# A decoder step with two attentions, a mixture of low-rank experts and a quantised MLP on one core: score products by halves, keys by DMA, and all MLP inputs kept

## The chip, the cores and the metric

The kernel runs on one core of a Trainium2 chip. The metric is the device time of one execution in microseconds (us). A hand-written order for every engine is part of the program; the engines only meet at semaphores.

## The reference

Sixteen sequences of 128 positions with 256 features, all independent, go through five stages (`b` is the sequence, called a block below):

```python
a  = attention0(q=LN(x), k=ctx, v=ctx)         # 16 heads of 16, causal, softmax over 128 positions
x  = x + a
xh = LN(x)
x  = x + xh @ base_w.T + base_b + 2 * sum_e gate_e * (xh @ A_e) @ B_e   # top 2 of 8 experts, rank 16
q  = LN(x)
x  = x + gamma * attention1(q, ctx, ctx)       # over the features: 8 heads of 16 positions, 256 x 256 scores
xn = rmsnorm(LN(x)) * g
h  = gelu(bit_linear(xn, w1))                  # 256 -> 1024; inputs rounded to 8 bits, weights to -1, 0, 1
x  = x + bit_linear(h, w2)                     # 1024 -> 256
```

The second attention works on each block turned on its side: its positions are the 256 features, and its 8 heads have 16 of the 128 sequence positions each.

## The kernel before, in words

**Work of a block.** A head has only 16 rows to sum over, so scores are made with 32 rows of the systolic array at a time: `R = 32`, four row tiles `i = 0..3`, each with two heads (`E = 2`) side by side. The keys are kept with the rows of the other head set to zero: `k0` and `k1` hold for each `e` the 32 rows times the 0/1 column `keep[:, e]`. `place_k0` (L2348 to L2358) and `place_k1` (L2360 to L2371) make them on VectorE from `kv_in`, two `tensor_scalar` each per block.

A score is made twice. `scores0` (L1028) makes it with queries on partitions: four mask products by `mask_rows` (L1036), then the q by k product (L1046). `maxima0` (L2151) takes the row maximum on VectorE (L2154), negated. GpSimd splits the maxima in two bf16 halves (`split_max0`), TensorE turns them (`turn_max0`, L1058), ScalarE copies them (`copy_max0`), and `scores0_t` (L1062) makes the scores again with keys on partitions (L1071) and adds the negated maxima by a product with ones (L1076). ScalarE takes the exponential (`exp0`, L1662), GpSimd zeroes what the mask hides (`mask0`, L583), and `pv0` (L1125) multiplies by the values. The second attention has the same parts with a 1 for the 0: `scores1` (L1082, product L1090), `maxima1` (L2158, L2161), `turn_max1`, `scores1_t` (L1106, L1114 and the ones at L1119), `exp1` (L1710), `pv1` (L1139). It has no mask and twice the columns: its calls have two indices, `f` (or `k`) for half of the 256 columns and `h` for the half of the row tiles.

**Halves.** Every score call works on one half `h`: row tiles 0 and 1, or 2 and 3, in PSUM banks `at` and `at + 1`. `together(a, b)` (L1017) interleaves the matmuls of two calls on different halves, so that four row tiles are at work; a call given alone uses two. A block has 2 `scores0`, 2 `scores0_t`, 4 `scores1` and 4 `scores1_t`, so 192 calls in all; 130 of them stand in 65 pairs.

**The expert stage.** `turn_xh1`, `ff` (L1176, product L1182: base weights, all A and the router in one), `logits_`, `top_`, `index`, `gate1_`, `pick`, `gates_`, `gated_` on VectorE, `turn_gated`, `lora` (L1193), `moe_out`.

**The second attention's denominators.** They stand in the rows of `u1`, four heads apart, and are brought to the right rows through HBM by SyncE (SP): `save_u1` (L360) writes `u1`, `close_z1` (L366, two DMAs) reads back the denominators, `rz1_` (L2247) inverts them on VectorE, `save_rz1` writes them, `spread_rz1` (L389) reads them spread over the rows, and `close_u1` (L376, two DMAs) reads the sums. `a1_` (L645, GpSimd) multiplies the two, and `out_` (L2253) adds it to the stream. All of SP's instructions wait in program order.

**The MLP.** `xn_`, `amax_in`, `scale_in`, `round_in` (ScalarE), `quant_in`, `turn_in`, `copy_in` prepare a block's input `xq_t`; there are `XT_BUFS = 7` buffers. `up` (L1206), `gelu` (L1741), `amax_hid`, `keep_amax_hid` (GpSimd), `scale_hid`, `round_hid`, `quant_hid`, `turn_hid`, `copy_hid`, `down` (L1225), `scale_output`, `add_output` and `store_out` follow. The gelu needs another activation table than the exponential, so the MLP comes after all the attention work: inputs 0 to 6 are made before it, 7 to 15 in it. Its hidden rows have their own buffer `hid`, and the MLP weights come in f32 into `w1_sb` and `w2_sb`, are summed (`weight_sum`), rounded on ScalarE (`round_weight`) and clipped (`clip_weight`) among the first blocks.

**Order.** Each engine's program is a flat list of calls, written out from L410 (SP), L699 (GpSimd), L1233 (TensorE), L1768 (ScalarE) and L2385 (VectorE). From block 4 of the expert stage on it repeats. One turn of TensorE's list is, for instance:

```python
turn_xh1(8, 7); pv0(9, 0, 6); pv0(9, 1, 6)
together(scores0_t(9, 0, 0), scores1(5, 1, 1, 2)); turn_in(2, 7); ff(8, 6); turn_q0(12, 5)
together(scores1_t(4, 0, 0, 0), scores0(11, 1, 2)); turn_u0(9, 7); turn_max1(5, 5); pv1(4, 0, 4)
together(scores1(6, 0, 1, 0), scores1_t(5, 1, 0, 2)); pv1(4, 1, 4); turn_gated(8, 7)
together(scores1(6, 0, 0, 0), scores1_t(5, 1, 1, 2)); together(scores1(6, 1, 0, 4)); lora(8, 6)
turn_max0(10, 7); together(scores0(11, 0, 0), scores1_t(5, 0, 1, 2)); together(scores0_t(10, 1, 4))
```

(It is condensed to several calls on a line, with a label or two moved to one turn.) It has five pairs and two single calls.

Of the kernel before, what the change touches and what calls it, by code (L numbers as in the profile page):

```python
# [55 lines left out]
XT_BUFS = 7  # L56
HID_BUFS = 7
CONSTS = 15
TURNS = 4
# [22 lines left out]
def program(nc, x, kv, w_ff, base_b, router_b, lora_b, attn_gamma, w1, w2, mlp_gamma, out):  # L82
    with ExitStack() as ctx:
# [17 lines left out]
        ones_bf = sb("ones_bf", [P, P], BF16)  # L101
        warm = sb("warm", [P, 1])
# [4 lines left out]
        keep = sb("keep", [P, E])  # L107
        attn_gamma_all = sb("attn_gamma_all", [P, 1])
        mlp_gamma_all = sb("mlp_gamma_all", [P, D])
        w1_sb = sb("w1_sb", [P, FT * HID])  # L110
        w2_sb = sb("w2_sb", [P, HT * D])
# [8 lines left out]
        k0 = sb("k0", [P, K0_BUFS, FT, E, P])  # L120
# [70 lines left out]
        hid = sb("hid", [P, HID_BUFS, HID])  # L191
# [26 lines left out]
        kv_landed = [sem(f"kv_landed{n}") for n in range(KV_BUFS)]  # L218
        keep_ready = sem("keep_ready")
        k0_placed = sem("k0_placed")  # L220
        k1_placed = sem("k1_placed")
        v0_ones = sem("v0_ones")
# [112 lines left out]
        def _(sp):  # L335
# [74 lines left out]
            load_kv(0)  # L410
            load_kv(1)
            load_x(0)
            load_x(1)
            load_x(2)
            load_kv(2)
            load_weight(0)
            load_x(3)
            load_weight(1)
            load_x(4)
            load_x(5)  # L420
            load_constants()
            load_kv(3)
            load_kv(4)
            load_kv(5)
            load_kv(6)
            load_kv(7)
            load_kv(8)
            save_u1(0)
            close_z1(0)
            close_u1(0)  # L430
            save_rz1(0)
            spread_rz1(0)
            load_kv(9)
            save_u1(1)
            close_z1(1)
            close_u1(1)
            save_rz1(1)
            spread_rz1(1)
            load_kv(10)
            save_u1(2)  # L440
            close_z1(2)
            close_u1(2)
            save_rz1(2)
            spread_rz1(2)
            load_kv(11)
            save_u1(3)
            close_z1(3)
            close_u1(3)
            save_rz1(3)
            spread_rz1(3)  # L450
            load_kv(12)
            save_u1(4)
            close_z1(4)
            close_u1(4)
            save_rz1(4)
            spread_rz1(4)
            load_kv(13)
# [2538 lines left out]
```

## Time and profile before

| what | value |
|---|---|
| three runs | 369.82, 373.1 and 378.56 us; median 373.1 |
| the profiled execution | 373.23 us |
| its span, first to last instruction | 371.2 us, so 2.0 us lie around it |
| TensorE busy | 327.1 us (88%) |
| VectorE busy | 291.4 us (78%) |
| ScalarE busy | 234.1 us (63%) |
| GpSimd busy | 202.5 us (55%) |
| mean granted TensorE clock | 0.974 of 2.4 GHz |

The busy time of an engine is the union of its instructions' times. Durations below are of this one execution. A row of a timeline that says x8 is a run of eight instructions merged, and its two numbers are the start of the first and the time to the end of the last. Each f32 product shows as two records, one for each of its passes.

### The profile page before, as it was taken

The page shows a single profiled execution, that of the slowest core. Times are in us where ns is not written, and L with a number is a line of the kernel's source. Part 1 is how long each engine was busy: PE and PEld are TensorE (multiplying, and loading weights), DVE is VectorE, ACT ScalarE, POOL GpSimd, SP SyncE. Part 2 cuts the span into 40 slices and gives each one's busy share as a digit, 9 for nine tenths or more (in the row PEclk, how much of TensorE's full clock was granted, in tenths as well). Part 3 has the DMA queues.
Part 4 walks back from the last instruction along what each step waited for, and adds up shares of the span by engine and source line. Part 5 has one row for each costly group of instructions (what it writes and reads, how often), then busy time and mean ns, then how long its engine had stood idle before and what let it go on. Part 6 is the DMA issues. An engine that isn't in the chain of part 4 may idle for free.

```text
span 371.2 us, 10692 instructions
## 1 busy us (share of the span) xinstructions
PE 327.1 (88%) x3730; PEld 211.8 (57%) x3730; DVE 291.4 (78%) x691; ACT 234.1 (63%) x373; POOL 202.5 (55%) x443
## 2 busy tenths in 40 slices
PE   0799799899999999989999999989999999498774
PEld 0477556557566666657666575756645563265543
DVE  6784786886869888888989888786887755689992
ACT  1225535347575676757576675656656669689992
POOL 7537784545355647564654747555643332455554
PEclk9999969899999999999999999999999999889998
DMA  7900211000212120221112021011111112021111
GB/s 246 354 26 3 63 52 29 2 3 2 58 33 59 33 72 18 75 55 51 59 32 65 26 74 44 24 40 31 47 44 32 48 58 61 17 77 52 45 57 57
DMA packets 20276, 20.61 MB, mean 56 GB/s; under 512 B 6016, under 2 KB 15872, under 8 KB 20224
## 3 DMA queue, kind: packets, MB, share of 16 engines
q1 hardware_dynamic: 20224, 19.94, 17.4%
q8 instruction: 30, 0.49, 0.6%
q14 instruction: 22, 0.18, 0.2%
HBM read 13.51 MB, written 6.42 MB: 54 GB/s over the span
## 4 chain that ended last, share of the span: by engine, by line
PE 47%; DVE 18%; issue 12%; DMA 11%; POOL 4%; ACT 4%; SPq 1%; POOLq 0%; DVEq 0%; ACTq 0%
PE ps L1090 6%; PE ps L1071 5%; PE ps L1114 5%; PE ps L1182 5%; PE ps L1046 4%; DMA u_kept<-u 4%; DMA rz_kept<-rz 4%; PE ps L1036 4%; DVE max L2161 3%; PE ps L1134 3%; DVE max L2154 2%; PE ps L1195 2%; PE ps L1147 2%; PE ps L1229 2%; ACT p L1710 2%
## 5 line engine op out<-in xcount | busy, mean ns | idle before, releaser
L1710 ACT ACTIVATE p<-ps 128x1024 f32<-128x1024 f32 x64 | 65.0, 1024 | 57.7 <-PE ps L1119 57.3
L2161 DVE TENSOR_REDUCE max<-ps 128x4 f32<-128x1024 f32 x64 | 76.9, 1219 | 14.6 <-PE ps L1090 14.5
L1090 PE MATMUL ps<-k,q 32*128 32x512 f32 x256 | 66.0, 641 | 6.9 <-DVE max L2161 4.8
L1114 PE MATMUL ps<-q,k 32*128 32x256 f32 x512 | 70.6, 398 | 0.6 <-DVE max L2161 0.5
L2154 DVE TENSOR_REDUCE max<-ps 128x8 f32<-128x1024 f32 x32 | 38.8, 1217 | 14.2 <-PE ps L1046 14.2
L1114 PEld LDWEIGHTS ps<-q,k 32*128 32x128 f32 x512 | 44.4, 184 | 8.6 <-issue 3.3
L1662 ACT ACTIVATE p<-ps 128x1024 f32<-128x1024 f32 x32 | 32.6, 1018 | 20.2 <-PE ps L1076 20.0
L583 POOL TENSOR_SCALAR_AFFINE_SELECT p<-p 128x1024 f32<-128x1024 f32 x32 | 35.2, 1100 | 13.4 <-ACT p L1662 13.2
L1046 PE MATMUL ps<-k,q 32*128 32x256 f32 x256 | 39.9, 444 | 1.8 <-DVE k L2357 1.8
L1071 PE MATMUL ps<-q,k 32*128 32x128 f32 x512 | 38.0, 297 | 0.4 <-DVE max L2154 0.4
L1147 PE MATMUL ps<-p,v 128*32 128x256 f32 x512 | 34.3, 384 | 3.5 <-ACT p L1710 3.5
L1071 PEld LDWEIGHTS ps<-q,k 32*128 32x128 f32 x512 | 34.3, 203 | 3.9 <-DVE max L2154 2.1
L1090 PEld LDWEIGHTS ps<-k,q 32*128 32x128 f32 x256 | 19.3, 183 | 17.2 <-issue 7.4
L1046 PEld LDWEIGHTS ps<-k,q 32*128 32x128 f32 x256 | 24.8, 214 | 3.8 <-DVE k L2357 2.0
L1036 PE MATMUL ps<-mask_rows,ident_rows 32*128 32x512 bf16 (+3 forms) x256 | 26.1, 328 | 0.5 <-ACT p L1710 0.2
L649 POOL TENSOR_TENSOR a<-uz,rz_all 128x256 f32<-128x256 f32 x16 | 11.7, 733 | 26.8 <-issue 26.8
L1182 PE MATMUL ps<-wff_sb,xh_t 128*128 128x392 f32 x64 | 26.1, 532 | 0.0
L1229 PE MATMUL ps<-w_q,hq_t 128*128 128x256 bf16 x128 | 18.0, 287 | 8.1 <-DVE hq_t L2335 6.6
L1147 PEld LDWEIGHTS ps<-p,v 128*32 128x32 f32 x512 | 14.4, 109 | 18.4 <-issue 12.3
L1119 PE MATMUL ps<-max_t,ones_bf 2*128 2x512 bf16 x128 | 24.9, 376 | 0.0
L612 POOL TENSOR_SCALAR var<-mv 128x1 f32<-128x1 f32 x32 | 7.6, 239 | 30.3 <-DVE mv L2245 20.1
L1754 ACT ACTIVATE hr<-hid,round_all,qscale 128x1024 f32<-128x1024 f32 x16 | 20.0, 1250 | 4.9 <-DVE qscale L2323 3.3
(134 smaller groups left out, 727.4 us busy)
## 6 DMA issues: line engine op xcount, KB each, us to landing
kv_in<-in_kv SPq DMA_DIRECT2D x16, 256.0 KB, 2.8
u_kept<-u SPq DMA_DIRECT2D x16, 256.0 KB, 3.1
w_sb<-in_w SPq DMA_DIRECT2D x4, 512.0 KB, 7.6
uz<-u_kept SPq DMA_DIRECT2D x32, 64.0 KB
rz_all<-rz_kept SPq DMA_DIRECT2D x16, 128.0 KB
out<-xs SPq DMA_DIRECT2D x16, 128.0 KB, 1.7
xs<-in_x SPq DMA_DIRECT2D x1, 768.0 KB, 10.3
xs<-in_x SPq DMA_DIRECT2D x2, 256.0 KB, 5.8
```

The source lines that it names most:

```text
L583: pool.affine_select(out=kept, in_=kept, compare_op=ALU.is_ge, fill=0.0, base=0, pattern=[[0, HALF * FT * E], [1, P]], channel_multiplier= ...
L1036: pe.matmul(heads, ident_rows[rows, a, :], mask_rows[rows, a, a * R:P].unsqueeze(1).broadcast_to([R, FT * E, P - a * R]), start=(a == 0), ...
L1046: last = pe.matmul(ps[:, at + m, f * D:(f + 1) * D], q0[rows, b % Q_BUFS, f, :], k0[rows, n, f, :, :].rearrange("p e l -> p (e l)"), start ...
L1071: pe.matmul(ps[:, at + m, c * P:(c + 1) * P], k0[rows, n, f, e, :], q0[rows, b % Q_BUFS, f, :], start=(c == 0), stop=True, skip_group_chec ...
L1090: pe.matmul(ps[:, at + m, :], q1[rows, b % Q_BUFS, f * P:(f + 1) * P], k1[rows, n, :, :].rearrange("p e l -> p (e l)"), start=True, stop=True,
L1114: pe.matmul(ps[:, at + m, e * D:(e + 1) * D], k1[rows, n, e, k * P:(k + 1) * P], q1[rows, b % Q_BUFS, :], start=(e == 0), stop=True, skip_ ...
L1147: last = pe.matmul(ps[R * j:R * (j + 1), at, h * D:(h + 1) * D], v1[:, b % V1_BUFS, k * H1 + h * G + j, :], p1[:, k, h * HALF + m, e, :], ...
L1182: last = pe.matmul(ps[:, at, 0:NFF], xh1_t[:, f, :], wff_sb[:, f, :], start=(f == 0), stop=(f == FT - 1), skip_group_check=True)
L1662: act.activation(p0[:, b % 2, h * HALF:(h + 1) * HALF, :, :, :].rearrange("p i f e q -> p (i f e q)"), wide(at).rearrange("p m c -> p (m c ...
L1710: act.activation(p1[:, k, h * HALF:(h + 1) * HALF, :, :].rearrange("p i e q -> p (i e q)"), wide(at).rearrange("p m c -> p (m c)"), ACT.Ex ...
L2154: dve.tensor_reduce(max0[:, h * HALF:(h + 1) * HALF, :].rearrange("p i c -> p (i c)"), wide(at).rearrange("p m (c k) -> p (m c) k", k=P), ...
L2161: dve.tensor_reduce(max1[:, f, h * HALF:(h + 1) * HALF, :].rearrange("p i e -> p (i e)"), wide(at).rearrange("p m (e k) -> p (m e) k", k=D ...
```

## The change

It does five things, and orders all five engines' lists anew.

1. **First keys by DMA.** `place_k0` goes. Three `memset`s zero `k0` at the start; SP then loads each block's keys straight from HBM by two DMAs (`load_k0`), one for each head of a pair, each to every second partition of the 128, 1 KB a row. The layout of `k0` is now `[n, e, f, l]`, and the rows of the two heads alternate, so `norm0` writes its output permuted (stride of two elements), and the products read `k0[rows, n, :, f, :]`. A `load_k0(b)` waits until `scores0_t` of block `b - 3` is done with the buffer; `kv_in` no longer waits for `place_k0`.
2. **Second keys by one product.** `place_k1`'s two `tensor_scalar` of 256 columns become one `tensor_tensor` of 2 x 256, both operands broadcast.
3. **Halves in pairs in other places.** `together` is unchanged. The two halves of one `scores0` are paired for blocks 0 to 5 and 7, and sometimes two `scores1` or two `scores1_t` of different halves. The whole list has 63 pairs and 66 single calls. The products with ones stay, in `scores0_t` and in `scores1_t`.
4. **16 MLP inputs.** `XT_BUFS` goes from 7 to 16. To make room, `hid`, `w1_sb` and `w2_sb` share one buffer. Inputs 0 to 12 are turned before the first gelu (`round_in(13)` also stands before it), and 13 to 15 after it.
5. **SP.** x comes first, then the first keys, the constants, `kv_in` and the MLP weights; `close_u1` goes ahead of `close_z1`; `TURNS` (semaphores in rotation) goes from 4 to 3.

The diff, cut to its core (the lists show the start, one turn and the beginning of the MLP):

```diff
-XT_BUFS = 7
+XT_BUFS = 16
 HID_BUFS = 7
-TURNS = 4
+TURNS = 3
...
+        wide_rows = sb("wide_rows", [P, HID_BUFS * HID])
+        w1_sb = wide_rows[:, 0:FT * HID]
+        w2_sb = wide_rows[:, FT * HID:2 * FT * HID]
+        hid = wide_rows[:, :].rearrange("p (n c) -> p n c", c=HID)
...
-        k0 = sb("k0", [P, K0_BUFS, FT, E, P])
+        k0 = sb("k0", [P, K0_BUFS, E, FT, P])
...
-                    sp.wait_ge(k0_placed, (b - KV_BUFS + 1) * E)
-                    sp.wait_ge(k1_placed, (b - KV_BUFS + 1) * E)
+                    sp.wait_ge(k1_placed, b - KV_BUFS + 1)
...
+            def load_k0(b):
+                n = b % K0_BUFS
+                if b < K0_BUFS:
+                    sp.wait_ge(k0_zeroed, b + 1)
+                else:
+                    for h in range(2):
+                        sp.wait_ge(st0_ready[h], (b - K0_BUFS + 1) * HALF)
+                heads = kv[b, :, 0, :].rearrange("(i e d) l -> e i d l", e=E, d=DH)
+                for e in range(E):
+                    sp.dma_start(k0[e:P:E, n, e, :, :].rearrange("p f l -> p (f l)"), heads[e]).then_inc(k0_landed[n], 16)
...
+            load_x(0); load_x(1); load_x(2); load_k0(0); load_x(3); load_k0(1); load_k0(2); load_constants()
+            load_x(4); load_kv(0); load_kv(1); load_x(5); load_kv(2); load_weight(0); load_weight(1)
...
+            save_u1(4); load_kv(12); close_u1(4); close_z1(4); load_k0(12); save_rz1(4); spread_rz1(4)
...
-                pe.wait_ge(k0_placed, (b + 1) * E)
+                pe.wait_ge(k0_landed[n], (b // K0_BUFS + 1) * E * 16)
...
-                                         k0[rows, n, f, :, :].rearrange("p e l -> p (e l)"), start=False, stop=True,
+                                         k0[rows, n, :, f, :], start=False, stop=True,
...
+            together(scores0(0, 0, 0), scores0(0, 1, 2)); turn_q0(1, 7); turn_max0(0, 7)
+            together(scores0(1, 0, 0), scores0(1, 1, 2)); together(scores0_t(0, 1, 4)); together(scores0_t(0, 0, 0))
+            turn_q0(2, 7); turn_max0(1, 7); together(scores0(2, 0, 0), scores0(2, 1, 2)); ...
...
+            together(scores1_t(4, 0, 0, 0), scores0(9, 1, 2)); pv0(8, 0, 6); pv0(8, 1, 6); pv1(4, 0, 5)
+            turn_max1(5, 4); turn_u0(8, 6); together(scores1_t(5, 1, 0, 0), scores1(6, 1, 1, 2))
+            turn_gated(7, 4); turn_max0(9, 6); pv1(4, 1, 5)
+            together(scores1(6, 1, 0, 0), scores1_t(5, 0, 1, 2)); together(scores1(6, 0, 0, 4)); lora(7, 7)
+            together(scores1_t(5, 1, 1, 0), scores0(10, 0, 2)); together(scores0_t(9, 1, 4)); turn_xh1(8, 7)
+            together(scores1(6, 0, 1, 0)); together(scores0_t(9, 0, 2)); ff(8, 7); turn_in(3, 6); turn_q0(11, 5)
...
-                normalise(xh0[:, :], stream(b), rstd0[:, b:b + 1], shift0[:, b:b + 1]).then_inc(norm0_done, 1)
+                turns = xh0[:, :].rearrange("p (t d e) -> p t e d", e=E, d=DH)
+                normalise(turns, stream(b).rearrange("p (t e d) -> p t e d", e=E, d=DH), rstd0[:, b:b + 1],
+                          shift0[:, b:b + 1]).then_inc(norm0_done, 1)
...
-                for e in range(E):
-                    dve.tensor_scalar(k1[:, n, e, :], kv_in[:, b % KV_BUFS, 1, :], keep[:, e:e + 1], 1.0, ALU.mult,
-                                       ALU.mult).then_inc(k1_placed, 1)
+                dve.tensor_tensor(k1[:, n, :, :], kv_in[:, b % KV_BUFS, 1, :].unsqueeze(1).broadcast_to([P, E, D]),
+                                  keep[:, :].unsqueeze(2).broadcast_to([P, E, D]), ALU.mult).then_inc(k1_placed, 1)
...
+            round_in(13); gelu(0, 0, 7); gelu(0, 1, 4); gelu(1, 0, 6); gelu(2, 0, 5); gelu(1, 1, 4); gelu(3, 0, 7)
+            round_hid(0)
```

In the list before, eight gelus stand ahead of `round_hid(0)`, and no `round_in` right ahead of them.

## Rows read from the trace of the kernel before

**Rows 1.** Busy time by stretch: PE, PEld, DVE, ACT, POOL, clock, DMA share, GB/s.

```profile
11.50:43.00 31.50, 30.85 (x262) 21.48 (x262) 21.42 (x47) 14.22 (x19) 16.34 (x34) 1.00 0.30 97
43.00:55.30 12.30, 10.29 (x111) 6.58 (x112) 11.34 (x30) 4.07 (x7) 10.78 (x19) 0.72 0.26 65
55.30:106.00 50.70, 47.88 (x581) 31.36 (x577) 38.28 (x84) 28.94 (x49) 23.93 (x52) 0.97 0.07 19
106.00:237.60 131.60, 125.94 (x1704) 85.02 (x1702) 111.36 (x287) 89.79 (x150) 79.69 (x177) 1.00 0.17 49
237.60:309.70 72.10, 67.37 (x730) 39.94 (x728) 51.64 (x133) 45.74 (x68) 32.89 (x77) 1.00 0.15 46
309.70:371.20 61.50, 44.76 (x358) 27.46 (x354) 48.66 (x93) 49.20 (x78) 30.11 (x62) 0.93 0.14 48
```

**Rows 2.** Timeline of PE in one turn of the repeating part.

```profile
198.12 0.59 PE L1090 MATMUL ps<-k,q 32*128 32x512 f32 x2
...
199.08 0.70 PE L1195 MATMUL ps<-lora_b_sb,gated_t 128*128 128x256 f32 x2
...
201.12 0.27 PE L1071 MATMUL ps<-q,k 32*128 32x128 f32 x2
...
202.33 0.44 PE L1165 MATMUL ps<-ident,xh 128*128 128x128 f32 x2
...
203.71 0.38 PE L1071 MATMUL ps<-q,k 32*128 32x128 f32 x2
...
205.02 0.28 PE L1202 MATMUL ps<-ident_bf,xq 128*128 128x128 bf16 x2
```

**Rows 3.** Timeline of PE: `ff` of blocks 4 and 12.

```profile
105.99 1.58 PE L1182 MATMUL ps<-wff_sb,xh_t 128*128 128x392 f32 x4
...
237.62 1.58 PE L1182 MATMUL ps<-wff_sb,xh_t 128*128 128x392 f32 x4
```

**Rows 4.** Timeline of PE: its longest wait in the turn of rows 2.

```profile
197.16 0.70 PE L1090 MATMUL ps<-k,q 32*128 32x512 f32 x2 [0.41 <-DVE max L2161]
```

**Rows 5.** Timeline of PE in the first 60 us.

```profile
35.73 1.25 PE L1036 MATMUL ps<-mask_rows,ident_rows 32*128 32x512 bf16 x8
36.77 2.02 PE L1046 MATMUL ps<-k,q 32*128 32x256 f32 x8
...
46.75 0.48 PE L1046 MATMUL ps<-k,q 32*128 32x256 f32 x2 [1.81 <-DVE k L2357]
...
55.83 1.08 PE L1046 MATMUL ps<-k,q 32*128 32x256 f32 x8
```

**Rows 6.** Timeline of DVE: a memset, and the first-key products.

```profile
4.92 1.34 DVE L2380 MEMSET v<- 128x1536 f32 x1 [0.27 <-issue]
...
45.48 1.21 DVE L2357 TENSOR_SCALAR k<-kv_in,keep 128x256 f32<-128x256 f32 x2
```

**Rows 7.** Groups of VectorE: xcount | busy, mean ns of one | idle before.

```profile
L2357 DVE TENSOR_SCALAR k<-kv_in,keep 128x256 f32<-128x256 f32 x32 | 15.8, 538 | 0.1
L2370 DVE TENSOR_SCALAR k<-kv_in,keep 128x256 f32<-128x256 f32 x32 | 11.5, 404 | 4.1 <-PE ps L1119 4.0
L2257 DVE TENSOR_TENSOR xs<-a,xs 128x256 f32<-128x256 f32 x16 | 7.4, 465 | 8.4 <-POOL a L649 8.4
```

**Rows 8.** Timelines of SP, POOL and ACT where the MLP begins.

```profile
310.75 1.08 SPq L382 DMA_DIRECT2D uz<-u_kept  x2
...
310.79 4.96 ACT L1747 ACTIVATE hid<-ps,dequant 128x512 f32<-128x512 f32 x8
...
317.43 0.72 POOL L649 TENSOR_TENSOR a<-uz,rz_all 128x256 f32<-128x256 f32 x1 [4.60 <-issue]
...
318.57 1.24 ACT L1754 ACTIVATE hr<-hid,round_all,qscale 128x1024 f32<-128x1024 f32 x1 [2.83 <-DVE qscale L2323]
```

**Rows 9.** A group of ScalarE (columns as rows 7); a DMA issue: KB, us to landing.

```profile
L1739 ACT COPY xq_t<-ps 128x256 bf16<-128x256 bf16 x16 | 5.8, 381 | 0.0
...
xs<-in_x SPq DMA_DIRECT2D x1, 768.0 KB, 10.3
```

More of the change, by code:

```diff
@@ new lines, in _ @@
+            together(scores0_t(4, 0, 0))
+            lora(1, 7)
+            together(scores1(0, 1, 1, 2), scores1(0, 1, 0, 4))
+            turn_q0(6, 6)
+            together(scores1(0, 0, 0, 0))
+            turn_max0(5, 7)
+            together(scores1(0, 0, 1, 4))
+            pv0(3, 0, 6)
+            pv0(3, 1, 6)
+            together(scores0(6, 0, 2), scores0_t(5, 1, 0))
+            turn_u0(3, 7)
+            turn_max1(0, 6)
+            together(scores1(1, 1, 1, 0), scores1(1, 1, 0, 4))
@@ new lines, in _ @@
+            turn_xh1(5, 6)
+            together(scores1_t(2, 1, 1, 0))
+            ff(5, 7)
+            together(scores1(3, 0, 1, 2), scores0_t(6, 0, 4))
+            turn_in(0, 6)
+            together(scores1_t(2, 0, 0, 0))
+            turn_max0(7, 5)
+            turn_q0(8, 6)
+            pv0(6, 0, 4)
+            pv0(6, 1, 4)
+            pv1(2, 0, 6)
+            turn_max1(3, 5)
+            turn_u0(6, 4)
+            together(scores1_t(3, 1, 0, 0), scores1(4, 1, 1, 2))
+            turn_gated(5, 5)
@@ L1395, in _ @@
-            together(scores0(11, 0, 0), scores1_t(5, 0, 1, 2))
-            together(scores0_t(10, 1, 4))
-            turn_xh1(8, 7)
+            pv1(4, 0, 5)
+            turn_max1(5, 4)
+            turn_u0(8, 6)
+            together(scores1_t(5, 1, 0, 0), scores1(6, 1, 1, 2))
+            turn_gated(7, 4)
+            turn_max0(9, 6)
+            pv1(4, 1, 5)
+            together(scores1(6, 1, 0, 0), scores1_t(5, 0, 1, 2))
+            together(scores1(6, 0, 0, 4))
+            lora(7, 7)
@@ L1416, in _ @@
-            together(scores0_t(11, 1, 4))
-            turn_xh1(9, 7)
+            pv1(5, 0, 5)
+            turn_max1(6, 4)
+            turn_u0(9, 6)
+            together(scores1_t(6, 1, 0, 0), scores1(7, 1, 1, 2))
+            turn_gated(8, 4)
+            turn_max0(10, 6)
+            pv1(5, 1, 5)
+            together(scores1(7, 1, 0, 0), scores1_t(6, 0, 1, 2))
+            together(scores1(7, 0, 0, 4))
+            lora(8, 7)
+            together(scores1_t(6, 1, 1, 0), scores0(11, 0, 2))
@@ L1425, in _ @@
[L1425 to L1437 removed]
+            pv1(6, 0, 5)
@@ new lines, in _ @@
+            turn_max1(7, 4)
+            turn_u0(10, 6)
+            together(scores1_t(7, 1, 0, 0), scores1(8, 1, 1, 2))
+            turn_gated(9, 4)
+            turn_max0(11, 6)
+            pv1(6, 1, 5)
+            together(scores1(8, 1, 0, 0), scores1_t(7, 0, 1, 2))
+            together(scores1(8, 0, 0, 4))
+            lora(9, 7)
+            together(scores1_t(7, 1, 1, 0), scores0(12, 0, 2))
+            together(scores0_t(11, 1, 4))
+            turn_xh1(10, 7)
+            together(scores1(8, 0, 1, 0))
@@ new lines, in _ @@
+            turn_u0(11, 6)
+            together(scores1_t(8, 1, 0, 0), scores1(9, 1, 1, 2))
+            turn_gated(10, 4)
+            turn_max0(12, 6)
+            pv1(7, 1, 5)
+            together(scores1(9, 1, 0, 0), scores1_t(8, 0, 1, 2))
+            together(scores1(9, 0, 0, 4))
+            lora(10, 7)
+            together(scores1_t(8, 1, 1, 0), scores0(13, 0, 2))
+            together(scores0_t(12, 1, 4))
+            turn_xh1(11, 7)
+            together(scores1(9, 0, 1, 0))
+            together(scores0_t(12, 0, 2))
@@ new lines, in _ @@
+            together(scores0_t(14, 1, 4))
+            turn_xh1(13, 7)
+            together(scores1(11, 0, 1, 0))
+            together(scores0_t(14, 0, 2))
+            ff(13, 7)
+            turn_in(8, 6)
+            together(scores1_t(10, 0, 0, 0), scores0(15, 1, 2))
+            pv0(14, 0, 6)
+            pv0(14, 1, 6)
+            pv1(10, 0, 5)
+            turn_max1(11, 4)
+            turn_u0(14, 6)
+            together(scores1_t(11, 1, 0, 0), scores1(12, 1, 1, 2))
+            turn_gated(13, 4)
```

2106 lines of the change are left out of this document (1008 added, 1098 removed).

## The prediction

> **What bounds the kernel now.** I read the busy table first: TensorE is busy for 88% of the span, VectorE for 78%, and no other engine for over 63%. An average over a start, a repeating part and an MLP says little, so the second view is the busy time by stretch [rows 1]. From 106 to 237.6 us TensorE works 125.9 of 131.6 us, and VectorE 111.4. In the MLP from 309.7 on it is ScalarE (49.2 of 61.5) and VectorE (48.7) that are full, and TensorE is not. In the first 55 us TensorE looks full as well, but its work is slow: eight q by k records take 2.02 us at 36.8 us and 1.08 us at 55.8 us [rows 5]. That is the 1.2 GHz level against the 2.4 GHz level. The granted-clock column does not show it in the stretch from 11.5 us to 43 us (it says 1.00) and shows it from 43 to 55.3 us as 0.72 [rows 1]; so I go by the durations.
>
> Third, the timeline of one turn of the repeating part [rows 2, 4]. Eight turns lie between the `ff` of block 4 and that of block 12 [rows 3]: 131.63 / 8 = 16.45 us a turn. TensorE idles (131.6 - 125.94) / 8 = 0.71 us of each [rows 1], 0.41 of it behind `maxima1` [rows 4]. TensorE therefore bounds the repeating part, with VectorE as its partner in a loop. What a freed VectorE can give back there is at most the 0.71 us a turn.
>
> **Part 1, first keys by DMA.** It takes 32 `tensor_scalar` off VectorE, 15.8 us in all [rows 7], about 1 us a block. In the repeating part that shortens nothing by itself, since TensorE is the bound. At the start it does: at 45.5 us the keys of blocks 3 to 5 stand in VectorE's queue [rows 6], and TensorE waits 1.81 us for them [rows 5]. Afterwards the clock falls back: 0.72 over 12.3 us means that 0.56 of it, 6.9 us, ran at half speed, some 3.4 us lost. With the wait gone I take back 1.8 us and a third of the 3.4, together -2.9 us; the bounds are 0 (another wait takes the place; the weight rounding and clipping move to this spot) and -5.2. What is added: three memsets of 512 columns, a third of 1.34 us each [rows 6], 1.3 us on VectorE while GpSimd is still building the masks, so nothing. `norm0` writes with a stride; ScalarE is idle for over a third of every stretch before the MLP, so nothing there either. Each block's two DMAs are issued by SP after `close_z1`, two turns before the keys are read. No row shows this DMA. The nearest are x's loads in the crowded first 20 us, the slowest of which took 10.3 us to land [rows 9]. The first keys are issued at about 3 us and wanted at about 12, so the bounds are 0 and +1.5; I take 0. A `load_k0` waits for `scores0_t` three blocks before, and behind it stand `save_rz1` and `spread_rz1`; those wait for the denominators anyway, which come 1 to 2 us later.
>
> **Part 2, second keys by one product.** Before, two of them cost 11.5 / 16 = 0.72 us a block [rows 7]. One product of 2 x 256 isn't in the trace. The nearest is a `tensor_tensor` of 256 columns, 0.465 us [rows 7]; the new one lies between that and twice that. I take the middle, 0.70: no change, bounds -0.25 and +0.21 us a block on an engine that isn't the bound.
>
> A rule speaks against this part. The Trainium skill, VectorE: DVE Perf Modes, section "Mode 2x_2P — use both read ports for one tensor", says that f32 `tensor_scalar` gets two elements a cycle from SBUF and `tensor_tensor` never does. The trace agrees in kind: 0.404 against 0.465 us for 256 columns [rows 7]. The same page gives (N + 151) / 0.96 ns for an f32 `tensor_tensor`, an estimate of 0.69 us here; the sum would not move by it.
>
> **Part 3, pairs in other places.** The number of score calls stays; 65 pairs become 63. At the start the two halves of `scores0` run as one. One half takes from 35.7 to 38.8 us at the slow clock [rows 5], 3.06 us, and a pair should take about as long. But the maxima, their split and the turn stand behind each, so TensorE idles after block 0's scores instead. Walking the new list with these durations I come to the turned maxima of block 2 at about 41 us in place of 43: -1.8 us, bounds -4 and 0.
>
> In the repeating part the new turn has four pairs and four single calls in place of five and two. A pair of `scores0_t` and `scores1` takes 205.02 - 203.71 = 1.31 us [rows 2]. Alone, `scores1` takes 199.08 - 198.12 = 0.96 and `scores0_t` 202.33 - 201.12 = 1.21 [rows 2]. In the new turn they follow each other on different halves, so the second pass of the first (0.48) can lie beside the second: 0.96 + 1.21 - 0.48 = 1.69, +0.38 us a turn, bounds 0 and +0.86 (no overlap). Against it stands the idle time. In the new order `turn_max0` and `pv1` lie between a `maxima1` and the claim of its bank, so the 0.41 goes; `turn_max1` now has only `turn_u0` between it and the product that needs its copy, which ScalarE makes after an exponential, a norm and a copy. I expect 0.25 us of waiting a turn there and nothing else: -0.46. Sum -0.08 a turn, eight turns: -0.6 us, bounds -3.7 and +5.
>
> From 55.3 to 106 us TensorE idles 50.7 - 47.88 = 2.8 us [rows 1] in much the same loops, with VectorE 76% full. A lighter VectorE gives a part of it back: -1 us, bounds -3 and +1. From 237.6 to 309.7 the idle 4.7 us [rows 1] come from waits for exponentials, which the change leaves: 0, bounds -2 and +1.
>
> **Parts 4 and 5, MLP and SP.** Six `copy_in` (blocks 7 to 12) leave the stretch in which ScalarE is the bound: 6 x 5.8 / 16 = -2.2 us [rows 9]. The MLP's first waits are given by SP, though: `a1_(14)` waits 4.60 us for its DMAs, `keep_amax_hid(0)` stands behind it on GpSimd, and ScalarE waits 2.83 us for the scale [rows 8]. The change issues `close_u1`, 1.08 us for its two DMAs [rows 8], ahead of `close_z1`, which is first in the chain of DMAs that ends last: +1.1. `out_(14)` goes ahead of `scale_hid(0)` on VectorE: +0.4. Eight gelus took 4.96 us ahead of the first rounding [rows 8]; now six stand there, so two come after the wait instead of beside it: +1.2. Sum +0.5 us, bounds -2.5 and +4; the upper one because `round_in(13)`, which needs `a1_(13)`, now stands ahead of the first gelu. `TURNS` = 3 only lengthens a wait that is three blocks old: nothing. The shared `hid` buffer adds no wait, for the weights are clipped 250 us before.
>
> **The sum.** -2.9 - 1.8 - 0.6 - 1.0 + 0 + 0.5 = -5.8 us. The profiled execution took 373.2 us, the same as the median of the three runs (373.1, which range from 369.8 to 378.6). Forecast: 367.5 us (the sum rounded), 1.5% faster. About 2% is what a measurement of this kernel can tell from no change.
>
> **Rivals.** (A) *Most of the idle time and all of the fall-back of the clock go.* The idle time from 43 to 309.7 us is 2.0 + 2.8 + 5.7 + 4.7 = 15.2 us [rows 1]; with half of it back, 3.4 us for the clock, 1.8 at the start, and the lost pair paid (+3), the time is 373.2 - 7.6 - 3.4 - 1.8 + 3.0 = 363.4. For it: VectorE has 1 us a block more slack, and most of TensorE's waits name VectorE. Against it: the repeating part idles only 4%. Chance 0.35.
>
> (B) *The repeating part gets longer.* The place is the product after `turn_max1`. If ScalarE is late there by one exponential (1.0 us) and the two single calls do not overlap (+0.86), a turn takes 16.45 + 1.0 + 0.86 - 0.41 = 17.9 us. Eight turns give +11.6, the start -2: 382.8. It decides from a turn of about 17.6 us on. For it: fewer pairs, and a wait with only 0.5 us of cover. Against it: ScalarE is 68% busy there [rows 1]. Chance 0.12.
>
> (C) *The change doesn't do all that it says.* The products of ones stay in the code, so no TensorE work goes; that is certain and is in my sum. Left over is the case in which the start gains nothing, because the maxima's chain and not the scores sets it, and the MLP loses 3 us to SP's chain: 373.2 - 0.6 + 3 = 375.6. Chance 0.10.
>
> My own case has 0.43, from 365 to 371. Over the cases: faster by over 2% (below 365.7) 0.37, within 2% 0.50, slower (above 380.6) 0.13. The range 359 to 377 leaves out most of B and the far end of A.
>
> **What would show the steps right or wrong.** The `ff` of blocks 4 and 12 should stand 131 us apart (129 to 135). The first should come at about 100.5 in place of 106.0. There should be no wait of TensorE for a key product near 45 us, and the clock of 43 to 55 us should be above 0.8. VectorE's busy time should fall by about 15 us, to 276, and the new key product should take about 0.70 us. From the first gelu to the end it should be about 60.5 us as before, with ScalarE's wait ahead of the first rounding longer than 2.8 us. I am wrong if a turn takes over 17 us, or if TensorE waits for key DMAs at the start.

## The result, and the profile after

The changed kernel takes 366.5 us (median of 20 runs, 364.3 to 374.1), the kernel before 371.8 us (20 runs, 368.4 to 384.3). The ratio is 0.984, with a 95% interval from 0.981 to 0.986: 1.6% faster. Eleven of the twenty runs of the changed kernel lie between 364.3 and 366.8 us and nine between 370.9 and 374.1; the ratio compares the faster group of the one kernel with that of the other. The forecast was 367.5 us, so the sum came out right. Its terms did not, as the profile shows at once. The profiled execution of the changed kernel has a span of 363.4 us, 7.8 less than before.

The first view is the busy time by stretch, with the columns of [rows 1]. The first two stretches are those of before, the third is six turns from the first product with the second values (`pv1`, line 1177) of block 3 to that of block 9, the last is from the first gelu to the end:

```profile
11.50:43.00 31.50, 26.07 (x368) 18.43 (x367) 23.30 (x44) 16.58 (x25) 23.60 (x46) 0.89 0.52 180
43.00:55.30 12.30, 9.62 (x115) 6.17 (x113) 10.49 (x32) 6.93 (x13) 7.48 (x13) 1.00 0.18 55
131.21:232.86 101.65, 97.46 (x1282) 64.71 (x1280) 81.36 (x199) 68.66 (x114) 60.15 (x132) 1.00 0.17 53
307.01:363.40 56.39, 40.21 (x345) 25.59 (x350) 46.34 (x81) 46.16 (x70) 27.00 (x58) 0.97 0.15 50
```

The same two last stretches of the kernel before, cut at its own marks:

```profile
143.57:242.09 98.52, 94.32 (x1275) 63.41 (x1275) 83.49 (x215) 66.68 (x111) 58.92 (x132) 1.00 0.17 49
310.79:371.20 60.41, 43.67 (x350) 26.95 (x348) 47.67 (x90) 48.12 (x77) 30.11 (x62) 0.93 0.15 49
```

Three things are to be seen. TensorE did 368 matmul records in the stretch from 11.5 to 43 us, in 26.1 us of busy time, where before it had done 262 in 30.9 [rows 1]: it is much faster there although it idles more. A turn then takes 101.65 / 6 = 16.94 us, against 98.52 / 6 = 16.42 before: the repeating part got longer by 0.52 us a turn. (`start_unpaired`, `save14_late` and `changed_again` have the same lists in this stretch and the same clock, and take 16.76, 16.98 and 16.99 us, so the tenth of a us is not firm.) The MLP takes 56.4 us in place of 60.4.

`pv1` comes once a block in both kernels and serves as a mark (its first half, start in us). Its place within a turn differs a little between the two orders, so single rows are good to some us:

| | block 0 | 3 | 6 | 9 | 12 | first gelu | end |
|---|---|---|---|---|---|---|---|
| before | 93.6 | 143.6 | 193.1 | 242.1 | 283.3 | 310.8 | 371.2 |
| after | 85.2 | 131.2 | 182.5 | 232.9 | 276.3 | 307.0 | 363.4 |
| lead | 8.4 | 12.4 | 10.6 | 9.2 | 7.1 | 3.8 | 7.8 |

The start gives 12.4 us by block 3, the rest of the attention gives 8.6 of them back, and the MLP adds 4.0. The timeline of TensorE tells of the start:

```profile
18.06 0.40 PE L1088 MATMUL ps<-ident_bf,max_split 128*128 128x128 bf16 x4 [2.69 <-POOL max_split L626]
19.09 2.04 PE L1076 MATMUL ps<-k,q 32*128 32x256 f32 x16
...
22.54 1.16 PE L1101 MATMUL ps<-q,k 32*128 32x128 f32 x16
...
27.29 1.94 PE L1076 MATMUL ps<-k,q 32*128 32x256 f32 x16
...
29.06 1.05 PE L1101 MATMUL ps<-q,k 32*128 32x128 f32 x16
...
40.07 1.08 PE L1076 MATMUL ps<-k,q 32*128 32x256 f32 x14
```

Both halves of a score, 16 records, take 2.04 us at the 1.2 GHz level, as long as one half of 8 records took before (2.02) [rows 5]. And the 2.4 GHz level comes sooner, though not at one stroke. The turn of 18.06 us is at it already (0.40 us, where the same four records take 0.61 at the lower level), the products from 19.09 on are at 1.2 GHz, those of 22.54 at 2.4, those of 27.29 at 1.2 again (1.94 us, against 1.08 at 40.07), and from 29.06 us on the level is 2.4 GHz up to about 121 us. Before, every record is long up to 41 us, and 20 records of the kind of 22.54 took 1.16 us only from 43.02 us on.

### The profile page after: what moved, and what is told of

Same layout as the page of the kernel before. It is cut to its first block, busy times and chain, and to the rows that moved or that the text cites. A ratio compares the mean times of both kernels' runs of the same rounds, so it can differ in the third digit from the quotient of the medians.

```text
span 363.4 us, 10645 instructions
## 1 busy us (share of the span) xinstructions
PE 316.9 (87%) x3724; PEld 200.9 (55%) x3730; DVE 282.5 (78%) x646; ACT 235.3 (65%) x373; POOL 203.8 (56%) x443
## 4 chain that ended last, share of the span: by engine, by line
PE 35%; issue 16%; DVE 15%; DMA 14%; POOL 9%; ACT 6%; SPq 4%; POOLq 0%; ACTq 0%; DVEq 0%
PE ps L1120 6%; DMA rz_kept<-rz 5%; PE ps L1144 5%; DVE max L2196 5%; DMA z<-u_kept 4%; DMA rz_all<-rz_kept 4%; PE ps L1177 4%; PE ps L1101 4%; PE ps L1212 3%; PE ps L1076 3%; SPq L396 2%; POOL a L679 2%; PE ps L1066 2%; PE ps L1164 2%; POOL rstd L643 1%
## 5 line engine op out<-in xcount | busy, mean ns | idle before, releaser
L1144 PE MATMUL ps<-q,k 32*128 32x256 f32 x512 | 66.1, 402 | 5.1 <-ACT max_t L1740 3.7
L1120 PE MATMUL ps<-k,q 32*128 32x512 f32 x256 | 63.8, 628 | 0.6 <-DVE max L2196 0.3
L1144 PEld LDWEIGHTS ps<-q,k 32*128 32x128 f32 x512 | 41.7, 185 | 18.3 <-issue 9.1
L1101 PE MATMUL ps<-q,k 32*128 32x128 f32 x512 | 36.5, 286 | 1.1 <-ACT max_t L1691 0.5
L1101 PEld LDWEIGHTS ps<-q,k 32*128 32x128 f32 x512 | 32.6, 195 | 3.6 <-ACT p L1697 1.5
L1076 PE MATMUL ps<-k,q 32*128 32x256 f32 x256 | 30.9, 445 | 0.0
L1259 PE MATMUL ps<-w_q,hq_t 128*128 128x256 bf16 x128 | 16.6, 272 | 10.4 <-DVE hq_t L2370 9.2
L1120 PEld LDWEIGHTS ps<-k,q 32*128 32x128 f32 x256 | 18.8, 183 | 11.5 <-issue 5.7
L1789 ACT ACTIVATE hr<-wide_rows,round_all,qscale 128x1024 f32<-128x1024 f32 x16 | 19.8, 1239 | 3.9 <-DVE hq L2364 3.5
L2345 DVE TENSOR_REDUCE amax<-wide_rows 128x1 f32<-128x1024 f32 x16 | 19.4, 1211 | 3.1 <-ACT wide_rows L1782 3.1
L1242 PE MATMUL ps<-w_q,xq_t 128*128 128x512 bf16 x58 | 17.5, 394 | 3.7 <-ACT wide_rows L1782 2.1
L1259 PEld LDWEIGHTS ps<-w_q,hq_t 128*128 128x128 bf16 x128 | 11.5, 97 | 16.8 <-DVE hq_t L2370 15.6
```

The source lines that it names most:

```text
L1076: last = pe.matmul(ps[:, at + m, f * D:(f + 1) * D], q0[rows, b % Q_BUFS, f, :], k0[rows, n, :, f, :], start=False, stop=True, skip_group_ ...
L1101: pe.matmul(ps[:, at + m, c * P:(c + 1) * P], k0[rows, n, e, f, :], q0[rows, b % Q_BUFS, f, :], start=(c == 0), stop=True, skip_group_chec ...
L1120: pe.matmul(ps[:, at + m, :], q1[rows, b % Q_BUFS, f * P:(f + 1) * P], k1[rows, n, :, :].rearrange("p e l -> p (e l)"), start=True, stop=True,
L1144: pe.matmul(ps[:, at + m, e * D:(e + 1) * D], k1[rows, n, e, k * P:(k + 1) * P], q1[rows, b % Q_BUFS, :], start=(e == 0), stop=True, skip_ ...
L1259: last = pe.matmul(ps[:, at, 0:D], hq_t[:, k, :], w2_q[:, k, :], start=(k == 0), stop=(k == HT - 1))
```

## The experiments

Twelve runs, in three sets; every set had its own runs of the kernel before on the same chip, and the ratios are to those. Differences of one experiment to the changed kernel are differences of ratios.

**1. The pairs of the start undone.** Six pairs of the changed kernel are taken apart (block 0 shown):

```diff
-            together(scores0(0, 0, 0), scores0(0, 1, 2))
+            together(scores0(0, 0, 0))
+            together(scores0(0, 1, 2))
```

> The changed kernel, with the two halves of the scores of blocks 0 to 5 one after the other again in place of in pairs. Theory 1 (the pairs bring TensorE's clock up early): in the changed kernel the full clock comes at 20.9 us, before it came at 43; without the pairs it comes 10 us or more later than 20.9, and the time grows by 5 to 9 us, to 368 to 372 on the changed kernel's 363.4 us span plus 1.8. Theory 2 (as predicted: only slow passes are saved, 1.8 us): the clock comes at about 21 us as in the changed kernel, or its rise changes nothing, and the time grows by 0 to 2.5 us.

Measured: 1.014 (1.008 to 1.020), which is 3.0% above the changed kernel; the span is 376.0 us, 12.6 more. TensorE's timeline:

```profile
20.60 2.12 PE L1076 MATMUL ps<-k,q 32*128 32x256 f32 x12
...
41.50 2.20 PE L1101 MATMUL ps<-q,k 32*128 32x128 f32 x32 [0.34 <-ACT max_t L1697]
...
50.08 2.12 PE L1076 MATMUL ps<-k,q 32*128 32x256 f32 x12
...
58.08 1.08 PE L1076 MATMUL ps<-k,q 32*128 32x256 f32 x10
```

Every record up to 54 us is at the slow level, those of 58 us are not. `pv1` of block 3 starts at 144.7 us, not at 131.2: one edit takes back the whole lead of the start and one us more. Theory 1 holds, and its price was set too low. The edit does two things at once, though: it lengthens the passes and it delays the clock. At the slow level the scores of block 0 end at 15.80 us where the pair ends at 14.75, so the passes are worth about 1 us a pair. By an estimate that is at most 6 of the 12.6 us, and the earlier clock is the rest; no run takes the two apart.

**2. First keys by DMA, alone.** The kernel before, with `load_k0`, the strided `norm0` and the zeroed buffers of the change, and without its 32 products for the first keys. In `before_k0_dma` the loads stood behind what was in SP's list; `before_k0_dma2` put two places right:

```diff
 # before_k0_dma2 against before_k0_dma
-            load_kv(8)
-            save_u1(0)
+            save_u1(0)
+            load_kv(8)
...
+            load_k0(3)
+            load_k0(4)
             load_kv(3)
             load_kv(4)
-            load_k0(3)
             load_kv(5)
-            load_k0(4)
             load_k0(5)
```

> The kernel before, with the first keys placed by two DMAs a block and the 32 products for them gone from VectorE; all orders otherwise as before. Theory 1 (as predicted): the wait of 1.81 us near 46.75 us goes and a part of the clock's fall-back with it, -2 to -5 us, the clock still comes up at about 43 us, and the turn stays at 16.45 us. Theory 2 (the order decides, not the keys): within 1.5 us of before. Theory 3 (the DMAs are what brings the start forward): the full clock comes 10 us earlier and 6 us or more are gained.

> The kernel before with the first keys by DMA, as in the run before_k0_dma, but with SP's list put right in two places: save_u1 ahead of the load_kv of its turn, and the first-key loads of blocks 3 and 4 ahead of load_kv(3), which waits for GpSimd. Theory 1 (the loss of 5.75% in that run came from SP's order, not from the DMAs): the wait of 3.13 us near 45 us goes, the turn is 16.3 to 16.6 us again, and the time is 0 to 5 us below that of the kernel before. Theory 2 (the two DMAs a block cost by themselves, 1.14 us of issue in SP's chain ahead of the denominators): the turn stays above 17 us and the time above 380 us.

Measured: 1.058 (1.051 to 1.064) for the first, 1.007 (1.004 to 1.010) for the second. The first kernel waits in both places. Its TensorE near 48 us and near 189 us, then SP's queue in that turn and at the start of the next:

```profile
48.59 0.80 PE L1074 MATMUL ps<-k,q 32*128 32x256 f32 x2 [3.13 <-DMA k<-in_kv]
...
189.24 0.30 PE L1218 MATMUL ps<-ident,gated 128*128 128x128 f32 x1 [2.33 <-DVE a L2202]
```

and

```profile
171.38 0.33 SPq L347 DMA_DIRECT2D kv_in<-in_kv  x1
171.80 0.38 SPq L376 DMA_DIRECT2D u_kept<-u  x1
...
178.07 1.14 SPq L359 DMA_DIRECT2D k<-in_kv  x2
179.26 0.45 SPq L399 DMA_DIRECT2D rz_kept<-rz  x1
182.38 0.61 SPq L407 DMA_DIRECT2D rz_all<-rz_kept  x1
...
190.42 0.33 SPq L347 DMA_DIRECT2D kv_in<-in_kv  x1
190.85 0.39 SPq L376 DMA_DIRECT2D u_kept<-u  x1
```

The store of the attention output (171.80, and 190.85 in the next turn) goes out only behind the key load of its turn (171.38 and 190.42), which waits for a free buffer; what it stores was copied by 169.85 and by 187.61. What comes of the first store is spread at 182.38; GpSimd's `a1_` idles 3.71 us up to 185.89 for it, VectorE 2.54 us for GpSimd, and TensorE 2.33 us for VectorE. With the two places right the turn is back at 98.78 / 6 = 16.5 us (`ff` of block 6 to that of block 12), and over its runs no time is gained: 0.7% above before, although the one profiled execution has a span of 367.0 us, 4 less than before. TensorE's wait for the keys is gone there, and another of the same length stands 3 us behind it:

```profile
49.32 0.44 PE L1193 MATMUL ps<-ident,xh 128*128 128x128 f32 x2 [1.78 <-ACT xh L1665]
```

So none of the three theories of the first run stood: the freed 1 us a block of VectorE was worth no more in the order of before than the added loads cost, and two unlucky places in SP's list, put right together, cost 5%, some 19 us. Theory 1 of the second run is right about the loss and wrong about the gain.

**3. The repeating part.** `singles_paired` puts two neighbouring single calls into one pair in seven turns; `both_early`, `q0_swap`, `max1_early` and `both_swap` move calls so that TensorE has work where it was held.

```diff
 # singles_paired
-            together(scores1(5, 0, 1, 0))
-            together(scores0_t(8, 0, 2))
+            together(scores1(5, 0, 1, 0), scores0_t(8, 0, 2))
 # max1_early (in both_early and both_swap too)
+            turn_max1(5, 4)
             pv1(4, 0, 5)
-            turn_max1(5, 4)
 # q0_swap and both_swap (both_early: the same with bank 5)
+            turn_q0(10, 6)
             together(scores1(5, 0, 1, 0))
             together(scores0_t(8, 0, 2))
             ff(7, 7)
-            turn_in(2, 6)
-            turn_q0(10, 5)
+            turn_in(2, 5)
```

> The changed kernel, with the single call of scores1(b, 0, 1) and that of scores0_t(b+3, 0) behind it made one pair in seven turns of the repeating part. Theory 1 (a single call costs TensorE the overlap of its second half): TensorE's busy time a turn falls from 16.23 by 0.3 to 0.5 us, seven turns give 2 to 3.5 us, the turn is 16.5 us. Theory 2 (the turn is set by the waits round it): the busy time falls, the idle time grows by as much, and the time stays within 1 us.

> The changed kernel with two calls of TensorE's list moved in the repeating part: turn_q0 of the next block ahead of the pair scores1(b, 0, 1), scores0_t(b+3, 0) in six turns, and turn_max1 ahead of pv1(b, 0) in eleven. Theory 1 (TensorE is held twice a turn: 0.30 us by VectorE's maxima0, whose two banks the second call of that pair claims, and 0.32 us by ScalarE's copy of the turned maxima): both go, a turn takes 16.1 to 16.3 us in place of 16.7, and the time falls by 3 to 5.5 us. Theory 2 (another loop of the turn is as long): the turn stays at 16.5 to 16.7 us and the time falls by 0 to 1.5 us.

> The changed kernel once more, as the measure for the three beside it. Every theory: 0.98 to 0.99 of the time before.

> The changed kernel with turn_max1 ahead of pv1(b, 0) in eleven turns, and nothing else moved. Theory 1 (ScalarE's copy of the turned maxima holds TensorE for 0.32 us a turn): the wait goes and the time falls by 1 to 3 us. Theory 2 (what is saved there is waited for at the next point of the turn: in both_early turn_max0 waited 0.5 to 0.9 us for VectorE's a0_, which the order before hid): a wait of 0.3 to 0.9 us ahead of turn_max0 in most turns, and the time is the same or up to 3 us longer.

> The changed kernel with turn_q0 ahead of the pair scores1(b, 0, 1), scores0_t(b+3, 0) in six turns as in both_early, where it waited 1.17 us for an exponential that held its bank 5; here it goes to bank 6, and turn_in to bank 5. Theory 1 (the 0.30 us for VectorE's maxima0 is a loss of TensorE that another task can fill): no wait ahead of turn_q0, the turn takes 16.4 us in place of 16.7 in these six, the time falls by 1 to 2.5 us. Theory 2 (the turn is a loop through VectorE and not TensorE's list): within 1 us.

> Both moves, with the banks exchanged: turn_max1 ahead of pv1(b, 0) in eleven turns and turn_q0 ahead of the pair in six. Theory 1 (both losses are TensorE's own): 2.5 to 5 us below the changed kernel, below every kernel of this study. Theory 2 (the loop through a0_ or the exponentials closes): not below it.

Measured: `singles_paired` 0.990 (0.984 to 0.996), with TensorE's busy time 16.23 us a turn as without the edit (both over the three turns from block 6 to 9, in which the clock is 1.00). The two single calls stand on different row tiles, and in the changed kernel they already lie side by side. What holds the second is VectorE. Its pass over the banks that the second call claims, and the two calls on TensorE, in the changed kernel:

```profile
192.09 1.23 DVE L2189 TENSOR_REDUCE max<-ps 128x8 f32<-128x1024 f32 x1
```

and

```profile
193.06 0.70 PE L1120 MATMUL ps<-k,q 32*128 32x512 f32 x2
193.37 0.49 PE L1101 MATMUL ps<-q,k 32*128 32x128 f32 x4
```

The pass ends at 193.32, and 0.05 us later the second call starts. Such a wait is in no table of waits, since TensorE is not idle.

`both_early` came to 1.024 (1.019 to 1.028). The bank that I gave `turn_q0` was still held by an exponential, which cost a wait in each of the moved turns. With the banks exchanged, `changed_again` 0.988 (0.980 to 0.995), `max1_early` 0.988 (0.984 to 0.993), `q0_swap` 0.987 (0.980 to 0.994), `both_swap` 0.990 (0.983 to 0.996): no difference among the four. `both_swap` has neither of the two holds any more, and a turn of 101.04 / 6 = 16.84 us. One turn of its TensorE and VectorE:

```profile
185.72 0.38 PE L1088 MATMUL ps<-ident_bf,max_split 128*128 128x128 bf16 x4 [0.92 <-DVE a L2207]
```

and

```profile
184.82 0.43 DVE L2292 TENSOR_TENSOR xs<-a,xs 128x256 f32<-128x256 f32 x1 [1.26 <-POOL a L679]
```

The saved time comes back whole, as a wait of `turn_max0` for VectorE's `a0_`, which stands behind `out_`, which waits for GpSimd's `a1_`. Theory 2 of the last three runs holds: the turn is not set by TensorE alone. What else sets it shows in the chain of work that ended last, here of the changed kernel (start, us, what):

```profile
190.74 0.49 POOL v L607
191.23 0.02 SPq L348
...
191.28 0.34 SPq L349
...
191.72 0.55 SPq L396
...
192.31 0.52 SPq L396
...
192.93 0.52 SPq L387
...
193.49 2.51 DMA z<-u_kept
...
196.02 0.26 DVE rz L2286
...
196.30 2.35 DMA rz_kept<-rz
...
198.67 1.90 DMA rz_all<-rz_kept
...
201.50 0.70 POOL a L679
...
202.23 0.04 DVE xs L2292
```

No TensorE stands in this excerpt, nor in the chain from 131 to 220 us. GpSimd's `place_v1` frees the buffer that SP's `load_kv` waits for; behind that stand `close_u1` (L396) and `close_z1` (L387); then come three DMAs one behind the other, `a1_`, `out_`, and VectorE's and GpSimd's work of the block, until `place_v1` is reached again. One lap of it, from one `rstd` of GpSimd (L643) to the next, takes 16.73, 17.83, 16.66 and 16.74 us (starts at 138.07, 154.80, 172.63, 189.29 and 206.03). Over the six turns the three DMAs alone are 35.2% of the chain, 6.0 us a turn:

```profile
by line: issue 16.0%; DMA z<-u_kept 12.9%; DMA rz_kept<-rz 12.0%; DMA rz_all<-rz_kept 10.3%; SPq L396 5.2%; POOL a L679 4.1%; DVE max L2196 3.8%; POOL rms L699 3.7%; POOL rstd L643 2.8%; SPq L387 2.5%; POOL v L607 2.4%; PE ps L1120 2.1%; DV
```

TensorE's own lap is hardly shorter. In `start_unpaired`, which has the same lists in this stretch, the chain runs through the DMAs up to 197 us and through TensorE and its short wait behind `turn_max1` from there on, from one `pv1` to the next in 16.68 and 16.59 us:

```profile
199.65 1.00 PE ps L1177 x16
...
216.33 1.00 PE ps L1177 x16
...
232.92 1.00 PE ps L1177 x16
```

So the new turn has two loops of nearly one length, and shortening either alone can give back a few tenths of a us a turn at most. That the loop through SP sets the turn is read from the chain and from `both_swap`; no run shortened it.

The same line of the kernel before, over its six turns, is led by TensorE's and VectorE's scores:

```profile
by line: issue 9.6%; PE ps L1090 8.3%; PE ps L1114 8.1%; DVE max L2161 6.9%; PE ps L1071 6.5%; PE ps L1182 5.6%; DMA rz_kept<-rz 5.1%; DVE max L2154 4.4%; DMA u_kept<-u 4.4%; PE ps L1134 4.1%; PE ps L1036 2.7%; PE ps L1195 2.6%; DVE a L2172
```

**4. Second keys by two products again.**

```diff
-                dve.tensor_tensor(k1[:, n, :, :], ..., ALU.mult).then_inc(k1_placed, 1)
+                for e in range(E):
+                    dve.tensor_scalar(k1[:, n, e, :], kv_in[:, b % KV_BUFS, 1, :], keep[:, e:e + 1], 1.0, ALU.mult,
+                                       ALU.mult).then_inc(k1_placed, 1)
```

> The changed kernel with the second keys placed by two tensor_scalar of 256 columns again in place of one tensor_tensor of 512. The one takes 0.77 us in the changed kernel's trace, the two took 0.72. Theory 1 (as predicted: the form does not matter, VectorE is not the bound): within 1 us of the changed kernel, VectorE's busy time less by about 0.7 us. Theory 2 (the pass of maxima0 that stands behind it in VectorE's list sets a wait of TensorE in every turn, so each 0.05 us counts, and two instructions release sooner or later than one): 1 to 3 us of difference to either side.

Measured: 0.998 (0.995 to 1.002), 1.4% above the changed kernel as first measured, and 1.1% above `changed_again`, whose interval (0.980 to 0.995) just touches this one. The profile gives no cause in the repeating part: a turn is 16.87 us (`pv1` of block 3 to that of block 9), and the span 365.1. What is longer is the MLP, 59.0 us in place of 56.4: the DMAs of block 14's residual landed later there and ScalarE waited 1.45 us ahead of its first rounding, not 0.46. Whether that belongs to the edit is open. The product itself is as forecast; the groups of VectorE in the changed kernel and in this run:

```profile
L2395 DVE TENSOR_TENSOR k<-kv_in,keep 128x512 f32<-128x512 f32 x16 | 12.2, 768 | 1.1 <-PE ps L1149 0.4
```

and

```profile
L2396 DVE TENSOR_SCALAR k<-kv_in,keep 128x256 f32<-128x256 f32 x32 | 12.1, 423 | 1.3 <-PE ps L1149 0.7
```

**5. The MLP.** One run delays the store of block 14's attention output, one gives ScalarE six more copies where the kernel before had its own.

```diff
 # save14_late, in save_u1
+                if b == 14:
+                    sp.wait_ge(exp1_done[0][1], 16)
 # six_copies_more, at four places of ScalarE's list in the MLP
             gelu(5, 1, 6)
+            spare_copy(0)
+            spare_copy(1)
```

> The changed kernel, with the store of block 14's second attention output held until the first exponential of block 15 is done, which is 3.3 us later than in the changed kernel's trace (302.6 in place of 299.3 us). Theory 1 (ScalarE's wait ahead of the first rounding is set by when this store goes out): the wait of 0.46 us grows to about 3.3, and the time grows by 2.3 to 3.3 us. Theory 2 (the MLP is shorter because six copies are out of it, and the store's place is hidden): the time grows by less than 1 us.

> The changed kernel with six more copies of 128 x 256 on ScalarE where the kernel before had six of its own in the MLP; what they write is read by nothing. Theory 1 (as predicted: ScalarE is the bound of the MLP, and the six copies taken out of it were worth their duration): with 0.2 to 0.38 us each the time grows by 1.2 to 2.3 us. Theory 2 (the MLP is set by waits between the engines, and single copies fall into them): less than 0.7 us.

Measured: 1.002 (0.998 to 1.005) for the late store, 1.8% above the changed kernel. From the first gelu to the end it takes 60.6 us, and ScalarE's first rounding, beside that of the changed kernel:

```profile
316.50 1.24 ACT L1791 ACTIVATE hr<-wide_rows,round_all,qscale 128x1024 f32<-128x1024 f32 x1 [3.67 <-DVE qscale L2360]
```

and

```profile
311.05 1.24 ACT L1789 ACTIVATE hr<-wide_rows,round_all,qscale 128x1024 f32<-128x1024 f32 x1 [0.46 <-DVE qscale L2358]
```

The wait grew by 3.2 us and the MLP by 4.2: theory 1, and the price is 1.3 us for each us of this wait. In that price is a slower TensorE, whose granted clock in the MLP is 0.93 here and 0.97 in the changed kernel. (The span grew by 6.3 us; the other 2.1 lie ahead of the MLP, 1.7 of them already by `pv1` of block 3, long before the edited store.) The six copies gave 0.991 (0.988 to 0.994). By the ratio that is 0.8% above the changed kernel as first measured and 0.4% above `changed_again`; in the trace ScalarE is busy 1.5 us longer in the MLP and the MLP is 0.4 us longer (56.8), since waits behind VectorE take the copies in. That is one execution against one, and its clock was up late at the start (last section). The trace speaks for theory 2, the ratios leave room for up to 3 us.

## Why the prediction was right, and where it was not

The total was right by luck: the start gave far more than forecast, the rest of the attention took most of it back, and the MLP gave 4 us where a loss stood in the sum.

**Part 1, first keys by DMA: predicted -2.9 us, wrong.** The step "with the wait gone I take back 1.8 us and a third of the 3.4" stands on a wait that does go, but alone in the order of before the whole part measures +0.7% (run 2): another wait took its place, 1.78 us for ScalarE at 49.32, which the prediction had only as its bound of 0. The clock does fall back less there (0.86 from 43 to 55.3 us, before 0.72), and over the runs the time is not shorter for it. "ScalarE is idle for over a third of every stretch before the MLP" was misread too: from 106 to 237.6 us it is 32% [rows 1]. It was also called safe for the wrong reason: "behind it stand `save_rz1` and `spread_rz1`; those wait for the denominators anyway". The chain above shows them on the path, and the list with the loads in unlucky places cost 5.8%.

**Part 2, the one product: right.** It has a median of 0.69 us (forecast 0.70), a mean of 0.77. By the Trainium skill, VectorE: DVE Perf Modes, section "The TRN2 errata — SBUF-src ops pay a fixed extra latency per instruction", (N + 151) / 0.96 ns give 0.69 us for 512 columns; the median agrees, the mean does not, as single ones took up to 1.29 us. That it has no effect is not shown, since run 4 lies between.

**Part 3, the start: predicted -1.8 us (and -1.0 for 55 to 106 us), measured some -12 in the profiled execution.** I priced the new list at the old clock: "a pair should take about as long. But the maxima, their split and the turn stand behind each". Both halves of that are true in the trace (2.04 us for a pair, waits of 2.69 and 1.42 us behind the split). The failed step is the clock, taken as given until 43 us. Run 1 shows that with the pairs the full clock is first there at 18 us and stays from 29 us on, and without them comes at 55; the pairs are worth 12.6 us of span, shorter passes and earlier clock together.

**Part 3, the turn: predicted -0.08 us, measured +0.5.** The two terms on TensorE came out well: its busy time a turn is 97.46 / 6 = 16.24 us against 15.72, so +0.52 where I had +0.38 within 0 and +0.86; the wait behind `turn_max1` is 0.32 us, forecast 0.25. The idle time did not fall: 0.70 us a turn as before. The 0.41 behind `maxima1` did go, and waits of `turn_max0` for VectorE's `a0_` took its place, 2.0 us over the six turns. The step that failed is the sum of the idle time ("0.25 us of waiting a turn there and nothing else"), and under it "TensorE therefore bounds the repeating part". In the changed kernel TensorE is not the only bound: a loop through SP's queue, three DMAs, GpSimd and VectorE is as long as the turn, and what TensorE saves comes back (`both_swap`). TensorE's own lap of 16.6 us would have missed the forecast as well, by 0.25 us a turn. It was rival B in its sign, with another mechanism, and I had no rival for SP's chain outside the MLP, though I had priced `close_u1` ahead of `close_z1` at 1.1 us there. Rival A was right that the clock had more to give than I took, though its place was the first 43 us and not the fall-back behind. The blocks behind were mis-sized too: from `pv1` of block 9 to the first gelu it takes 74.2 us, before 68.7, where I said 0. How much of these 5.5 us is only another place of `pv1` in the turn is not settled.

**Parts 4 and 5, the MLP: predicted +0.5, measured -4.0.** "So two come after the wait instead of beside it: +1.2" assumed that block 14's residual comes as late as before. The new order does `pv1` of block 14 earlier: its output is copied 8.3 us ahead of the first gelu, before 6.4 us, and SP's queue is free when it comes (0.6 us from copy to store, before 2.1). So the wait of 2.83 us [rows 8] fell to 0.46. At 1.3 us a us that is 3.1 of the 4.0; the copies, predicted to be worth 2.2, are worth 0.4 in the trace. The step that failed is the time at which block 14's residual comes.

Of the checks that I announced: no wait for a key product near 45 us and a clock above 0.8 there, both so; VectorE's busy time 282.5 us, forecast 276, partly since the new product took 12.2 us in all and not 11.2, and the 16 casts of the rounded MLP rows 13.4 and not 12.0; `ff` of block 4 and block 12 stand 133.3 us apart, inside the 129 to 135 that I had given, but `ff` of block 4 moved within its turn and tells nothing of the start. The MLP was to be 60.5 us with a longer wait: wrong on both counts.

## What to carry to other kernels

Where matmuls run at half speed, try another order of the same calls and look at when the durations fall: here pairing six calls was worth 12.6 us of span, by the estimate above twice the passes it saves. Before calling the busiest engine the bound, follow the longest chain of DMAs that closes from one turn to the next and write its length beside that engine's busy time; here they were 16.7 to 17.8 us and 16.2, or 16.6 with TensorE's own short wait, so that no edit to TensorE's list alone could show. What is still to be tried for that reason is SP's order itself (`close_z1` ahead of `close_u1`, `load_k0` behind `spread_rz1`); it was not tried, and no version of this study beats the changed kernel.

## What the runs showed of the hardware that I had not expected

TensorE's clock did not rise for being busy alone. Before, the engine has no gap from 15 to 25 us and hardly one up to 41, and its records are at the 1.2 GHz level throughout; in the changed kernel it is idle for 2.69 us ahead of 18.06, and the records of 18.06 are at 2.4 GHz. The pause is not what does it. In three other executions of the same list the level is up before the pause (the transpose of 14.7 us takes 0.44 us in place of 0.69), and in four it is low on both sides of it (the turn of 18.06 takes 0.61). With the six pairs taken apart every record is at the slow level up to 54 us. What the pairs change is that four row tiles work side by side from the first score on. That alone is not enough: the 32 records of 41.50 in `start_unpaired` are a pair too, and the level stays low for another 13 us. Which feature of the order brings the clock up is therefore not shown.

The order does not fix it either. Ten profiled executions have TensorE's list of the changed kernel in the first 60 us. In seven of them the 2.4 GHz level stays from 28.6 to 31 us on; in three (`max1_early`, `q0_swap`, `six_copies_more`) the granted clock is 0.50 from 25 to 41.5 us, and `pv1` of block 3 starts at 138.0 to 138.6 us, where in the seven it starts at 130.1 to 136.0. So the lead of 12.4 us is that of one execution: it is 7.6 to 13.5 us in the seven and 5.0 to 5.6 in the three.

The column of the granted clock reads 1.00 through the slow stretch of the kernel before [rows 1] and up to 55 us in `start_unpaired`. In the changed kernel it reads 0.50 from 19 to 21 and from 27 to 29 us, as the durations do. In these traces it agrees with the durations only from the first 2.4 GHz records on.

Two calls on different row tiles overlap on TensorE when they merely follow each other in its list. A `scores1` and the `scores0_t` behind it need no interleaving for it (16.23 us a turn both ways), and a busy engine can hide that the second is being held. The two halves of `scores0` do need it: one after the other they take from 11.68 to 15.80 us in `start_unpaired`, as a pair from 11.68 to 14.75 in the changed kernel, both at the 1.2 GHz level.
